# A decoder tower with experts: routing one causal group at a time instead of all tokens at the end

## The reference

```python
logits = (x @ w_g).reshape(N, E)
_, topk_idx = jax.lax.top_k(logits, K)
hot = jax.nn.one_hot(topk_idx, E, dtype=jnp.int32)
exp_mask = hot.transpose(1, 0, 2)
exp_rank = jnp.cumsum(exp_mask.reshape(K * N, E), axis=0) - 1
...
exp_mask = exp_mask * (exp_rank < cap).astype(jnp.int32)
...
h = jax.nn.gelu(jnp.einsum('ecd,edf->ecf', xb, fc_w) + fc_b, approximate=False)
out = jnp.einsum('ecf,efd->ecd', h, pj_w) + pj_b
y = jnp.einsum('nec,ecd->nd', cb_weight, out)
```

## Time and profile before

| | us |
|---|---|
| median of 3 runs | 1158.53 |
| lowest, highest | 1155.88, 1169.5 |
| the profiled execution, its own time | 1146.91 |
| its span in the trace | 1145.2 |

### The profile page before, as it was taken

One profiled execution on the slowest core, in us unless ns is written; L12 is line 12 of the kernel. 1 busy time (PEld: TensorE's weight loads), 2 busy tenths in 40 slices (PEclk: granted clock), 3 DMA queues, 4 the chain that ended last, 5 costly groups with the idle time before them and its releaser, 6 DMA issues.

```text
span 1145.2 us, 22242 instructions
## 1 busy us (share of the span) xinstructions
PE 961.2 (84%) x7330; PEld 736.5 (64%) x7330; DVE 662.2 (58%) x3059; ACT 692.0 (60%) x1515; POOL 465.5 (41%) x508
## 2 busy tenths in 40 slices
PE   2157989889889879999999998744999999999996
PEld 1144666556556546666666666533789898888886
DVE  1335788878877677777777656374334434333331
ACT  2014888887888788877887778434443443444342
POOL 5666664455001101122222212214266557657653
PEclk7576999999999889999999999955899999999999
DMA  7222121121000000010111011145464436545442
GB/s 203 42 39 45 32 39 26 25 39 26 1 1 2 1 1 2 2 34 3 32 33 34 2 34 34 33 88 83 73 89 85 99 76 87 100 71 112 54 51 28
DMA packets 58115, 53.33 MB, mean 47 GB/s; under 512 B 14462, under 2 KB 52256, under 8 KB 58016
## 3 DMA queue, kind: packets, MB, share of 16 engines
q0 software_dynamic: 26112, 27.89, 18.0%
q1 hardware_dynamic: 31904, 24.20, 7.7%
HBM read 35.67 MB, written 16.39 MB: 45 GB/s over the span
## 4 chain that ended last, share of the span: by engine, by line
PE 63%; ACT 11%; DVE 10%; issue 6%; POOL 6%; DMA 3%; POOLq 0%; ACTq 0%; DVEq 0%
PE ps_scores L695 12%; PE ps_ring L687 11%; PE ps_ring L695 10%; PE ps_ring L930 9%; PE ps_scores L804 6%; PE ps_ctx L821 5%; POOL got L518 4%; PE ps_scores L807 3%; PE ps_scores L930 3%; ACT probs L1039 2%; DVE probs L1301 2%; ACT x_full L1125 1%; DMA got<-word_table,id_now 1%; ACT probs L1136 1%; PE ps_ring L764 1%
## 5 line engine op out<-in xcount | busy, mean ns | idle before, releaser
L1136 ACT ACTIVATE probs<-ps_scores,fc_bias 128x512 f32<-128x512 f32 (+1 forms) x144 | 88.4, 617 | 160.9 <-PE ps_scores L695 156.7
L569 POOL DMA_INDIRECT out<-z_t,slots_now x80 | 129.9, 1623 | 115.0 <-DVE z_t L1583 93.7
L1021 ACT ACTIVATE prob_t<-ps_ring 128x512 f32<-128x512 f32 x192 | 114.4, 598 | 37.2 <-PE ps_ring L687 35.7
L687 PE MATMUL ps_ring<-ident,probs 128*128 128x128 f32 x768 | 122.1, 283 | 8.6 <-ACT k L988 3.5
L930 PE MATMUL ps_ring<-work,probs 128*128 128x192 f32 x672 | 117.1, 328 | 7.0 <-ACT probs L1136 7.0
L1047 ACT ACTIVATE probs<-probs,neg_max 128x128 f32<-128x128 f32 x384 | 120.6, 396 | 2.7 <-DVE neg_max L1301 2.7
L1030 ACT ACTIVATE square<-ps_scores 128x512 f32<-128x512 f32 x192 | 104.7, 600 | 27.5 <-PE ps_scores L804 12.3
L1301 DVE CUSTOM_DVE_ANT_0 probs<-ps_scores,causal 128x128 f32<-128x128 f32 x384 | 88.7, 286 | 53.5 <-PE ps_scores L807 53.1
L930 PEld LDWEIGHTS ps_ring<-work,probs 128*128 128x128 f32 x672 | 109.4, 190 | 10.4 <-issue 10.4
L695 PE MATMUL ps_ring<-x_hi,w_hi 128*128 128x512 f32 x208 | 93.0, 447 | 23.7 <-DVE k L1223 11.6
L695 PE MATMUL ps_scores<-x_hi,fc_hi 128*128 128x512 f32 (+1 forms) x288 | 104.8, 370 | 7.9 <-DVE x_hi L1567 7.9
(11 more groups left out here) (214 smaller groups left out, 2239.8 us busy)
## 6 DMA issues: line engine op xcount, KB each, us to landing
work<-pj_w SPq DMA_DIRECT2D x8, 576.0 KB, 4.5
token_in<-xin SPq DMA_DIRECT2D x8, 384.0 KB, 3.4
out<-resid SPq DMA_DIRECT2D x8, 384.0 KB, 4.2
vals<-fc_w SPq DMA_DIRECT2D x8, 384.0 KB, 3.3
vals<-fc_w SPq DMA_DIRECT2D x16, 192.0 KB, 4.2
out<-z_t,slots_now POOLq DMA_INDIRECT x80, 3.6
token_in<-xin SPq DMA_DIRECT2D x8, 128.0 KB, 4.6
got<-pj_b SPq DMA_DIRECT2D x8, 96.0 KB, 7.0
```

Source lines behind the costliest of these rows:

```text
L569: gp.indirect_dma_start(out[:, :], bass.IndirectOffsetOnAxis(slots_now[:, u, 1, t:t + 1], 0), slot_y[:, o, :], None, compute_op=ALU.add).t ...
L687: return pe.transpose(dst, src, ident[0:n, 0:n])
L1021: sc.activation(prob_t[:, s % 2, :, :], src.rearrange("p (h q) -> p h q", h=4), ACT.Exp if p is mag else ACT.Copy).then_inc(ring_free[i], 1)
L1136: sc.activation(hidden[:, c % 2, f_, 0:128 * nt], ps_scores[:, i, 0:128 * nt], ACT.Gelu, bias=fc_bias[:, e, f_:f_ + 1]).then_inc(gelu_done ...
```

## The change

Routing is cut into one batch per causal group, and the last group (number 15) into two: tiles 0 to 2, and tile 3. A batch has four parts. `mark_choices` (DVE, right after the logits of its last tile) writes the batch's one-hot rows. A fill "rank" (PE, two slots later) counts, for each pair, the pairs of the same expert ahead of it, with the counts of all earlier batches carried in `hots[:, 0]`. `place_pairs` (DVE, at that fill) makes ranks, slots, `low_hot` and `high_hot` in one block of 33 instructions for eight pairs. A fill "map" (PE, two slots after "rank") multiplies them, and DVE adds the product to `slot_map` in SBUF. First and second choices are counted apart, and a second choice's slot is counted down from the last slot of its expert; the second choices that meet occupied slots are masked with `used`, which the last batch makes from the counts of first choices. For number 15 the fills come one slot after the logits and one slot after each other.

After the last batch only five small steps stand ahead of `slot_src`. ACT no longer scales in a loop; it computes one small exponential a batch. POOL makes the constants (`count_up`) after pass 7. SP stores the weights of a group as soon as they are made, inside its loop over groups, and what it issues after that loop (biases, `fc_w`, `pj_w`) comes after the last batch's weights. The buffers lie in `square`, which the causal passes don't use.

```diff
+BATCHES = lambda number: ((0, 3), (3, 4)) if number == 2 * GROUPS - 1 else ((0, 4),)
+ROUTE_LAG = {"rank": 2, "map": 4}
+LAST_ROUTE_LAG = {"rank": 1, "map": 2}
...
+        if g is not None and g >= GROUPS:
+            some += [(g, f) for f in route_fills(g, STEPS * (p - g - 1) + slot)]
...
+                sp.wait_ge(weights_made, g + 1)
+                    sp.dma_start(rows_[:, :, 256:ROW], weight[:, bass.ds(GROUP * g, GROUP), :]).then_inc(weights_stored, 16)
...
+                elif kind == "map":
+                    pe.wait_ge(hots_made, batch_no(number, s))
+                    for k in range(TOPK):
+                        for t in range(end - first):
+                            last = pe.matmul(dst[:, 2 * HIGH * k:2 * HIGH * (k + 1)], low_hot[:, TOPK * t + k, :],
+                                             high_hot[:, TOPK * t + k, :, :], start=(t == 0), stop=(t == end - first - 1),
...
+            def place_pairs(no, b, i, n, src):
...
+                ve.tensor_tensor(low_hot[:, 0:pairs, :], number.unsqueeze(1).to_broadcast([128, pairs, LOW]),
+                                 low.unsqueeze(2).to_broadcast([128, pairs, LOW]), ALU.is_equal)
+                for c in range(pairs):
+                    t = tt.start + c // TOPK
+                    ve.tensor_scalar(high_hot[:, c, 0, :], number[:, 0:HIGH], high[:, c:c + 1], place_in,
+                                     ALU.is_equal, ALU.mult)
+                    last = ve.tensor_scalar(high_hot[:, c, 1, :], number[:, 0:HIGH], high[:, c:c + 1], 128.0 * t,
+                                            ALU.is_equal, ALU.mult)
+                last.then_inc(hots_made, 1)
...
-            for q in range(TOPK * SEQS // PAIRS_AT_ONCE):
-
-                act.wait_ge(ones_made, q + 1)
-                for j in range(PAIRS_AT_ONCE):
-                    c = PAIRS_AT_ONCE * q + j
-                    last = sc.activation(high_hot[:, q % HOT_RING, j, :], high_one[:, q % HOT_RING, j, :], ACT.Copy,
-                                         scale=token_no[:, c:c + 1])
-                last.then_inc(hots_made, 1)
```

More of the change, by code:

```diff
@@ L79, in due, with route_fills @@
     return k // 3 if k % 3 == 0 and 0 <= k // 3 < GROUP else None
+BATCHES = lambda number: ((0, 3), (3, 4)) if number == 2 * GROUPS - 1 else ((0, 4),)
+ROUTE_LAG = {"rank": 2, "map": 4}
+LAST_ROUTE_LAG = {"rank": 1, "map": 2}
+def route_fills(number, at):
+    some = []
+    for b, (first, end) in enumerate(BATCHES(number)):
+        for what in ("rank", "map"):
+            lag = (LAST_ROUTE_LAG if number == 2 * GROUPS - 1 else ROUTE_LAG)[what]
+            some += [(what, b)] if at == LAGS["logits"] + 3 * (end - 1) + lag else []
+    return some
 def causal_fills(at):
@@ new lines, in tower_kernel @@
+        rank_hot = of_square[:, 1680:1744].rearrange("p (c e) -> p c e", e=EXPERTS)
+        chosen, rank, slot_f, over = (of_square[:, 1744 + PAIRS * a:1744 + PAIRS * a + PAIRS].rearrange(
+            "p (t k) -> p t k", k=TOPK) for a in range(4))
+        at_i = of_square[:, 1776:1800].bitcast(I32).rearrange("p (a n) -> p a n", a=3)
+        at_f = of_square[:, 1800:1816].rearrange("p (a n) -> p a n", a=2)
+        in_expert = of_square[:, 1816:1816 + CAP_TILES]
+        place_in = of_square[:, 1826:1827]
@@ L454, in _ @@
                              resid[:, bass.ds(GROUP * g, GROUP), :]).then_inc(resid_stored, 16)
[L456 to L459, removed]
+                sp.wait_ge(weights_made, g + 1)
+                with nc.allow_non_contiguous_dma(reason="two weights a row"):
+                    sp.dma_start(rows_[:, :, 256:ROW], weight[:, bass.ds(GROUP * g, GROUP), :]).then_inc(weights_stored, 16)
             sp.wait_ge(cau.pv_done, JOBS * GROUPS + 2)
@@ L856, in _ @@
                 one_pass(p)
[L858 to L867, removed]
-                for j in range(PAIRS_AT_ONCE):
[L869 to L872, removed]
+            for i in range(RING):
+                pe.wait_ge(ring_free[i], (FILLS - i - 1) // RING + 1 + 1)
             for i in range(2):
@@ L971, in fill @@
                 src = ps_ring[:, i, :]
-                if kind in ("out", "logits", "ctx", "shift") or (kind == "value" and p is cau) or (
+                if kind == "rank":
+                    first, end = BATCHES(number)[s]
+                    tt = slice(GROUP * g + first, GROUP * g + end)
+                    act.wait_ge(gap_ready, batch_no(number, s))
+                    sc.activation(gap[:, 1, tt], gap[:, 0, tt], ACT.Exp).then_inc(gap_exp, 1)
+                if kind in ("out", "logits", "ctx", "shift", "rank", "map") or (kind == "value" and p is cau) or (
                         kind == "proj" and p is mag and s in DVE_PROJ):
@@ L1267, in fill @@
                     ve.max_index(best_at[:, t, :], best[:, t, :], logits[:, t, :]).then_inc(p.named("ordered"), 1)
+                    for b, (first, end) in enumerate(BATCHES(number)):
+                        if s == end - 1:
+                            mark_choices(number, b)
             def normalise_z(p, gb, s):
```

216 lines of the change are left out of this document (128 added, 88 removed).

## The result

| | us |
|---|---|
| kernel before, median of 4 runs beside it | 1157.2 |
| changed kernel, median of 4 runs | 1202.2 |
| ratio, 95% interval | 1.0416 (1.0354 to 1.0478) |
| changed kernel, profiled execution: own time, span | 1203.65, 1201.9 |

The account below looks back on a forecast made before the run. PE is busiest, but ahead of job 8 in the causal passes the chain of waits runs on DVE. Passes 43 us, plus clock 12, minus 15 at the end, gives +40 on 1158.53: 1198 us, range 1170 to 1215.

Parts of the forecast that it names:

- The block: DVE's routing work for eight pairs, ahead of job 8's maxima in passes 10 to 13: 6.3 us, 5.2 to 7.6.
- What of it reaches the pass: Passes 10 to 13: job 8 is 5.7 us late, with the map's addition 6.2 us a pass, 24.8 for four.
- the marking: DVE's one-hot rows two slots before the block: 0.55 us, of which 0.3 delays the pass.
- The map's addition: DVE adds the 320-column map product to the slot map once a batch: 0.5 us added to each pass.
- The clock: PE's stop in each of six passes lowers its clock: 2 us a stop, 12 in all, bounds 0 and 20.
- The second rival: Passes 10 to 15: the block delays but PE's clock stays up; +28 us, 1187 us; chance 22%.
- Passes 15 to 17: Routing adds 6.6 us in pass 15 and 5.7 in pass 16, plus one clock fall of 2 us.
- The end: From tile 2's logits to the first expert's first layer: 15 us shorter, bounds 11 and 17; slot_src at 18.0 us.
- the two would be level: At the end, the gather path (first layer at 38.2 us) and SP's bias and fc_w loads finish about together.
- the store would be a wait: At the end, POOL's gather waits for the last weights' store, taken as 4 us, and starts at about 20.5.
- The sum: Whole kernel: 43 us for passes plus 12 for clock minus 15 at the end, +40 on 1158.53: 1198 us.
- The first rival: Causal passes: the block hides in DVE's 10.9 free us, only the end changes; −15 us, 1144 us; chance 8%.

Follow-up runs that it names:

- The pieces at idle places: Changed kernel with each block of groups 8 to 14 cut into ten pieces, put where DVE waited in the kernel before: 1150.5 us, 0.9976.
- the matmuls in the wait: Changed kernel with 24 extra 128x128 matmuls, results unused, on PE ahead of job 9's scores in passes 10 to 15: 1192.3 us, 1.0294.
- the version with one last batch: Changed kernel, last group in one batch: 1198.5 us; where the first rival is discussed, that plus the pieces at idle places: 1149.3 us, again 1152.8 us.
- the control above: Kernel before the change with extra PE matmuls, results unused, in pass 16 and slots 0 to 9 of pass 17: 1158.7 us, 0.999.
- the ten pieces: Changed kernel with each block of groups 8 to 14 cut into ten pieces, one at the end of each slot from 10 on: 1167.3 us, 1.0079.
- the version with the memset: Changed kernel with one memset in place of the sixteen 80-column rows for groups 9 to 14, block 4.26 us: 1187.5 us, 1.0271.

## Why the prediction was right, and where its terms were off

The forecast of 1198 us was 4 us short of 1202.2, and the result lies in the range and on the forecast side. The mechanism is the one forecast: the block stands whole ahead of one row of maxima, PE stops, its clock falls. The pieces at idle places, which do the same DVE work, take away nearly all of the loss; the matmuls in the wait take away the clock's part; doubling the rows adds their length. How near the time came is in part luck, as the terms show:

- **The block.** Forecast 6.3, measured 6.86: small steps 1.98 (2.2), the 1024 columns 1.14 (1.2), the weights 0.52 (0.5), the sixteen rows 3.22 (2.4). The rows were mis-sized: they follow each other by 0.23 and 0.17 in turn, 0.20 on average, the upper bound given, and not 0.15.
- **What of it reaches the pass.** Job 8 in pass 12 starts 8.51 us after job 7 instead of 2.59, 5.9 late, against 5.4 (6.3 − 0.87; the 5.7 of the forecast has the marking in it). The marking lets 0.4 through (0.62 at job 6, of which 0.24 comes back at job 7), against 0.3. The map's addition was put at 0.5 and costs 1.1 even at full clock (job 9 to job 10: 3.77 instead of 2.66, with the matmuls in the wait): behind its 0.47 the norm waits 0.2 and then itself takes 0.4 longer. Together 7.4 a pass, 6.2 forecast.
- **The clock.** Forecast 2 a stop with bounds of 0 and about 3.3; measured 2.0 to 2.5 in four passes and 4.4 in one that had a second fall, or 1.7 to 2.4 in all five against the other profile of the same passes. The second rival, in which the clock stays up (1187 us), fell: behind a wait of 5.93 us the granted clock is 0.50, and it is 0.50 behind the block of 4.26 too. The Trainium skill's rule that DVE's copy out of PSUM between groups of matmuls does not cool PE ("TensorE: Matmul & The Clock Gate", "Loop structure matters more than you think") led to that rival; it does not carry over to DVE's work here, for which PE waits. With pieces at DVE's idle places, the clock of pass 13 stayed at 1.00.
- **Passes 15 to 17.** Forecast 14.3 (6.6, 5.7 and one stop), measured 17.2. One stop was too few: the clock is at its lower level for 42 us of this stretch (763.8 to 781.0, 787.8 to 794.5, 804.8 to the end) and was for 16 before. A single profile says little of the size: the version with one last batch, the same instructions up to tile 2's logits, took 86.57 us here, 24.0 more than before, at a mean clock of 0.66 against 0.73.
- **The end.** Forecast 15, measured 15.85, with two errors that nearly cancel. `slot_src` came 17.0 us after tile 2's logits (forecast 18.0), and the store of the last weights landed in 2.0 us, not 4 (nor within the bounds of 3 and 8.1), before POOL needed it: the first gather came at 18.2, not 20.5. But the first layer followed 19.5 us after it, not 17.7: PE waited for its rows until 854.81, 13.4 us behind the first gather instead of 11.6 (`fc_hi` waited for `fc_w` until 851.98). That the rows were held up by `fc_w`, issued 1.6 us after the first gather, is argued, not shown; the kernel before had a load of `fc_w` beside its gather too. In SP's part two more errors nearly cancel: the eight biases took 3.68 us to issue, not 8.0, and `fc_w` was there 8.9 us after its issue, not 5.1. That the two would be level was forecast; that the store would be a wait was wrong.
- **The sum.** Of the forecast's +55 for passes and clock the two profiles show 67.6, and of its −15 the end shows −15.9. By the medians the change costs 45 (41 to 55 by the interval), by the profiles 51 without the 5.5 ahead of pass 8, against a forecast of 40. The medians count; but the terms of the passes and the clock were too small by 12.6 together, and that the time still came within 4 us is in part luck. The profiled execution of the kernel before was a quick one, 1146.91 against the median of 1157.2: the control above, the same program up to pass 16, reached pass 8 at 440.76 instead of 428.35 in its profile.

The first rival (the block hides) fell because PE cannot go past job 9. Its arithmetic was not absurd: with the same DVE time at other places the pass comes to 39.5 us, and the version with one last batch comes out between 0.6% under and 0.2% over the kernel before in one comparison, and 0.04 to 0.8% under it in another.

## What to carry to other kernels

Free time of an engine in a stage is worth only what is idle at each place in its queue: look up the idle stretches of the engine in order, with what ended them, and cut added work so that each piece fits one, ahead of the instruction that waits there anyway. Where another engine is only one step ahead, as PE is here, a lump costs its length less the idle time at its place, and then the slower clock of the engine that it stops. And work taken from a serial end is only a gain after what it costs where it is put has been subtracted pass by pass: here, by the profiles, 16 us once against 68 us over the passes.

## What the runs showed of the hardware

**A per-partition scalar more costs time.** A row of 80 columns with two scalars per partition (L1571) keeps DVE for 0.23 us, one with a scalar and an immediate (L1573) for 0.17, seen in every block.

**DVE's rows stretch beside POOL's additions.** In pass 16 of the version with pieces at idle places, the timeline of DVE and POOL:

```profile
730.34 0.32 DVE L1593 TENSOR_SCALAR square<-square 128x80 bf16<-128x80 f32 x1
730.50 0.61 POOL L660 TENSOR_TENSOR resid<-resid,xin 128x192 f32<-128x192 f32 x1
730.57 0.60 DVE L1595 TENSOR_SCALAR square<-square 128x80 bf16<-128x80 f32 x1
731.09 0.48 DVE L1593 TENSOR_SCALAR square<-square 128x80 bf16<-128x80 f32 x1
...
731.48 0.59 POOL L660 TENSOR_TENSOR resid<-resid,xin 128x192 f32<-128x192 f32 x1
731.49 0.63 DVE L1595 TENSOR_SCALAR square<-square 128x80 bf16<-128x80 f32 x1
732.04 0.31 DVE L1593 TENSOR_SCALAR square<-square 128x80 bf16<-128x80 f32 x1
732.28 0.25 DVE L1595 TENSOR_SCALAR square<-square 128x80 bf16<-128x80 f32 x1
```

While POOL adds `xin` to `resid`, rows of 0.25 take 0.60 and 0.63, about as long as POOL's addition; after it they are back at 0.25. The same happens to the norm behind the map's addition in the version with matmuls in the wait (0.77 instead of 0.38, beside POOL's addition of 0.59). The Trainium skill, "SBUF — State Buffer", "Who interferes with whom", says that a DVE instruction in a two-port mode contends with GpSimd for a shared pair of ports: the one that issues first has it for its whole instruction, and the other blocks. The 0.60 and 0.63 agree with that; that these rows run in such a mode, no run here shows.

**The granted clock also falls without a long stop of PE.** The first maxima of pass 8 start between 427.3 and 441.3 us in the profiles of these kernels, whose earlier passes are the same. Where it is late, the clock fell more often on the way. In the trace of the ten pieces it is 0.53 from 174 to 181 us, with PE busy throughout; in the 4 us ahead PE had waited three times, the longest 1.25 us. In the trace of the version with the memset, whose program is the same here, it is 1.00 in these 7 us. The longest wait, and the stretch:

```profile
172.48 0.43 PE L875 MATMUL ps_ctx<-prob_t,work 128*32 128x128 f32 x8 [1.25 <-ACT prob_t L1065]
```

```profile
174.00:181.00 7.00, 7.00 (x45) 3.98 (x46) 3.33 (x19) 3.88 (x8) 0.00 (x0) 0.53 0.06 10
```

None of the kernels changes anything there, so these 14 us belong to none of the edits.
